# Three changes of order in a cross-attention and feed-forward kernel: weight requests ahead of context, six high halves on VectorE, first maxima earlier

## The reference, cut to what matters

```python
def reference(x, ctx, pweight, nweight, exps, bexps, mask_weight, scale, pbias, nbias, biasscale):
    x = x + attention(layernorm(x), ctx, ctx)        # causal, 16 heads, scale 1/8
    soft = sigmoid(pweight) - sigmoid(nweight)       # (1024, 1024, 4)
    weight = einsum('oin,n->oi', soft, exps * sigmoid(mask_weight)) * scale
    bias = quantised(einsum('on,n->o', pbias - nbias, bexps)) * biasscale
    return x + layernorm(x) @ weight.T + bias
```

## Time and profile before

| | us |
|---|---|
| median of 3 runs | 1187.38 (1184.31 to 1188.52) |
| the profiled execution, its own time | 1185.72 |
| its span | 1183.9 |
| TensorE busy | 1098.5 (93%) |
| VectorE busy | 994.4 (84%) |
| ScalarE busy | 862.3 (73%) |
| GpSimd busy | 492.7 (42%) |
| SyncE's transfers, share of 16 DMA engines | 70.4% |

### The profile page before, as it was taken

How to read it: one execution, slowest core, us unless ns; L and a number is a source line. 1 busy time by engine, 2 the same in 40 slices (tenths; PEclk the granted TensorE clock), 3 DMA queues, 4 the chain that set the end, 5 groups by cost and what they waited for, 6 DMA issues and landing times.

```text
span 1183.9 us, 32049 instructions
## 1 busy us (share of the span) xinstructions
PE 1098.5 (93%) x13092; PEld 808.7 (68%) x13092; DVE 994.4 (84%) x1552; ACT 862.3 (73%) x1770; POOL 492.7 (42%) x510
## 2 busy tenths in 40 slices
PE   3778888999999999999999999999999999999988
PEld 3666665666766777777776777777776676777753
DVE  5765688899988988998988888999988888998962
ACT  5887865777786777778776777777786777877740
POOL 3343534433334754344235654343335655331150
PEclk9999999999999999999999999999999999999999
DMA  8999936577659877775678887667768976654443
GB/s 308 301 295 337 299 80 120 134 146 122 151 121 186 189 180 131 162 160 112 132 121 203 194 173 148 139 140 130 137 125 205 185 171 131 137 117 86 89 90 71
DMA packets 382594, 191.13 MB, mean 161 GB/s; under 512 B 358128, under 2 KB 358128, under 8 KB 378352
## 3 DMA queue, kind: packets, MB, share of 16 engines
q1 hardware_dynamic: 381440, 189.05, 70.4%
q10 hardware_dynamic: 1008, 0.04, 0.1%
HBM read 67.15 MB, written 16.78 MB: 71 GB/s over the span
## 4 chain that ended last, share of the span: by engine, by line
PE 47%; DVE 18%; ACT 14%; DMA 7%; issue 7%; SPq 4%; POOL 3%; ACTq 0%; POOLq 0%; DVEq 0%
PE ffnb L468 15%; PE ptb L429 8%; PE slot L415 5%; PE slot L416 5%; DVE pd L656 4%; ACT p L537 4%; DVE mx L642 4%; DMA pd<-pd 4%; ACT pd L546 4%; PE obank L449 4%; ACT pt L553 4%; PE obank L452 3%; DVE stats L674 3%; PE obank L450 3%; DVE pt L648 3%
## 5 line engine op out<-in xcount | busy, mean ns | idle before, releaser
L537 ACT ACTIVATE p<-slot,mx 128x512 f32<-128x512 f32 (+7 forms) x512 | 377.4, 745 | 135.1 <-issue 71.2
L642 DVE TENSOR_REDUCE mx<-slot 128x1 f32<-128x640 f32 (+7 forms) x352 | 356.0, 1014 | 32.0 <-PE slot L419 31.3
L468 PE MATMUL ffnb<-wt,yt 128*128 128x512 f16 x1464 | 372.1, 380 | 1.1 <-DMA yt<-y 0.8
L648 DVE SCALAR_TENSOR_TENSOR pt<-ptb,pt 128x512 f16<-128x512 f32 (+1 forms) x504 | 281.6, 598 | 51.8 <-ACT pt L553 50.3
L553 ACT ACTIVATE pt<-ptb 128x512 f16<-128x512 f32 (+1 forms) x504 | 239.9, 526 | 106.0 <-PE ptb L429 104.8
L415 PE MATMUL slot<-kt,qt 128*128 128x128 f16 (+3 forms) x1056 | 267.2, 283 | 14.0 <-ACT p L537 5.9
L416 PE MATMUL slot<-kt,qs 128*128 128x128 f16 (+3 forms) x1056 | 267.2, 283 | 0.0
L870 POOL TENSOR_TENSOR ring<-ring,att 128x256 f32<-128x256 f32 x128 | 94.2, 736 | 394.0 <-DVE att L667 393.9
L429 PE MATMUL ptb<-id,p 128*128 128x128 f32 x1700 | 238.3, 279 | 10.9 <-DVE pt L648 10.8
L468 PEld LDWEIGHTS ffnb<-wt,yt 128*128 128x128 f16 x1464 | 137.2, 98 | 100.1 <-issue 2.2
L449 PE MATMUL obank<-v,pt 128*128 128x64 f16 x1700 | 176.9, 193 | 16.3 <-DVE att L667 12.1
(11 more groups left out here) (92 smaller groups left out, 1528.7 us busy)
## 6 DMA issues: line engine op xcount, KB each, us to landing
ring<-in_x_dram SPq DMA_DIRECT2D x32, 512.0 KB, 4.5
cin<-in_ctx_dram SPq DMA_DIRECT2D x32, 512.0 KB, 4.9
out_dram<-ring SPq DMA_DIRECT2D x32, 512.0 KB, 3.3
qs<-qt SPq DMA_DIRECT2D x124, 128.0 KB, 2.9
v<-in_weights_dram SPq DMA_DIRECT2D x11, 1024.0 KB, 8.1
kt<-in_weights_dram SPq DMA_DIRECT2D x11, 1024.0 KB, 8.0
pd<-in_weights_dram SPq DMA_DIRECT2D x5, 1024.0 KB, 7.3
yt<-in_weights_dram SPq DMA_DIRECT2D x5, 1024.0 KB, 10.0
```

Of the source, the lines that this page charges most:

```text
L468: last = pe.matmul(dst, yt[:, k % 2, a * KT_N + kk, :], wt[:, c, kk, half * 512:half * 512 + 512], start=r == 0, stop=r == 3 * KT_N - 1)
L537: last = nc.scalar.activation(p32[:, j.par, hh * j.keys:(hh + 1) * j.keys], slot[:, j.par, base:base + j.keys], ACT.Exp, bias=mx[:, j.par, ...
L642: nc.vector.tensor_reduce(mx[:, j.par, 0:j.heads], src[:, 0:j.heads, 0:j.keys], AX_X, ALU.max, negate=True).then_inc(mx_ready, 1)
L648: nc.vector.scalar_tensor_tensor(pt[:, j.par, j.blocks + blocks.start:j.blocks + blocks.stop, :], ptb[:, c % 2, 0:P * len(blocks)].rearran ...
```

## The change

It does three things. SyncE asks for a step's two chunks of weights before it asks for the context (and so also before turn_k), not after. For tiles 2, 3 and 4, VectorE writes the high halves of context and query itself, directly before the low halves, where ScalarE wrote them one or two steps earlier. In the prologue, ScalarE does the context's high half before the tanh of chunk 0, and takes the exponentials of job 0 before the query's high half and those of job 1 before the tanh of chunk 1; VectorE takes the maxima of job 0 before the context's low half, and those of job 1 before the query's.

```diff
+def high_on_dve(t):
+
+    return 1 < t < 5
...
                     if s == LOADS[n][0] and t + 3 < TILES:
                         load_x(t + 3)
+                    u = FIRST[t] + s + PAIRS // 2
+                    if u < UNITS:
+                        load_w(2 * u)
+                        load_w(2 * u + 1)
                     if s == LOADS[n][1] and t + 3 < TILES:
                         load_c(t + 3)
...
                     if s == turn_k_step(t) and t + 2 < TILES:
                         turn_k(t + 2)
-                    u = FIRST[t] + s + PAIRS // 2
-                    if u < UNITS:
-                        load_w(2 * u)
-                        load_w(2 * u + 1)
...
+            c_split(1)
             chunk_tanh(0)
-            c_split(1)
+            exponentials(JOBS[0])
             q_split(1)
+            exponentials(JOBS[1])
             chunk_tanh(1)
-            exponentials(JOBS[0])
-            exponentials(JOBS[1])
...
-                if s == C_HI[steps(t)] and t + 2 < TILES:
+                if s == C_HI[steps(t)] and t + 2 < TILES and not high_on_dve(t + 2):
                     c_split(t + 2)
-                if q_at(t, s, 2):
+                if q_at(t, s, 2) and not high_on_dve(t + 2):
                     q_split(t + 2)
...
             def q_split(t):
+                if high_on_dve(t):
+                    dve.wait_ge(q_norm, t + 1)
+                    dve.wait_ge(q_in[(t - 1) % 2], 16 * by_dma(t - 1))
+                    nc.vector.tensor_copy(q16[:, :, 0:D], norm32[:, :].rearrange("p (h d) -> p h d", d=D)
+                                          ).then_inc(q_hi, 1)
                 dve.wait_ge(q_hi, t + 1)
...
             def c_split(t):
+                v = v16[:, t % V_PLACES]
+                if high_on_dve(t):
+                    dve.wait_ge(c_in, 16 * (t + 1))
+                    nc.vector.tensor_copy(v[:, :, 0:D], cin[:, :].rearrange("p (h d) -> p h d", d=D)).then_inc(c_hi, 1)
                 dve.wait_ge(c_hi, t + 1)
...
+            maxima(JOBS[0])
             c_split(1)
+            maxima(JOBS[1])
             q_split(1)
-            maxima(JOBS[0])
-            maxima(JOBS[1])
             first_difference(0)
```

More of the change, by code:

```diff
@@ L692, in c_split @@
             def c_split(t):
+                v = v16[:, t % V_PLACES]
+                if high_on_dve(t):
+                    dve.wait_ge(c_in, 16 * (t + 1))
+                    nc.vector.tensor_copy(v[:, :, 0:D], cin[:, :].rearrange("p (h d) -> p h d", d=D)).then_inc(c_hi, 1)
                 dve.wait_ge(c_hi, t + 1)
-                v = v16[:, t % V_PLACES]
                 nc.vector.tensor_tensor(v[:, :, D:2 * D], cin[:, :].rearrange("p (h d) -> p h d", d=D),
```

## The result

| | before | after |
|---|---|---|
| median of the runs taken side by side, us | 1187.38 (1182.95 to 1188.95, 5 runs) | 1179.2 (1177.64 to 1184.74, 5 runs) |
| the profiled execution, its own time | 1185.72 | 1179.6 |
| its span | 1183.9 | 1177.8 |
| ratio after to before | | 0.9943, 95% interval 0.9921 to 0.9966 |

The changed kernel is 0.57% faster, 6.8 us with an interval of 4.0 to 9.4. The prediction was 1183.2, 4.2 us faster, which lies inside this interval. The two profiled spans are 6.1 us apart.

The account below looks back on a forecast made before the run. Bound: the saturated transfer queue with ScalarE nearly full at 76 to 142 us, TensorE from 200. Queue 2.3 + casts 1.9 + prologue and copies 0 = 4.2 us, giving 1183.2 from 1187.38; own range 1181.5 to 1185.0, wide 1180.0 to 1187.8.

Parts of the forecast that it names:

- That the stage decides and the rest follows: Weights stage, to about 150 us: ending it earlier moves all later work equally, so a gain there counts at the end.
- The prologue, 0: Prologue's new order: tile 2's load of x doesn't move, so earlier exponentials are waited off; 0, with 1 us either side.
- moments before 35 us: VectorE's moments of x of tile 2, at 36.01 before; starting before 35 us would prove the prediction wrong on the fast side.
- A transpose holds SyncE for the queue's sake, not for its own: SyncE's turn_k and turn_q: long durations of 7.25 to 11.03 us are the queue draining; an empty queue takes 1.78 us.
- The slower rival: Job 7: transposes keep their long times whatever is queued, chunk 22 is asked for later; 4.9 us slower, 1192.3, chance 0.09.
- The queue's gain, 2.3 us: Weights asked for ahead of context: chunks 22 and 23 gain what the saturated transfer queue gains, 2.3 us, bounds 0 and 5.7.
- two holes: Transfer queue empty about 1.3 us at 52 us, and about 1.0 us lost at 96 to 98 us inside a transpose.
- The wait for chunk 22: ScalarE, with stalls before chunks 18 to 21 gone, would wait the longer for chunk 22; its tanh near 109.4 us.
- The casts, 1.9 us from tile 4 and nothing from tiles 2 and 3: High halves moved to VectorE: tile 4's two save 2 x 0.95 us on the chain; the earlier four only lengthen ScalarE's wait.
- The copies meet GpSimd: Tile 4's copies on VectorE wait out a GpSimd neighbour, overdrawing their cover by about 1.4 us each; gain 1.4, 1186.0, chance 0.05.
- the wide range: Whole-kernel time of 1180.0 to 1187.8 us, taking in all cases but the fastest and slowest rivals, 0.17 together.
- the queue stops deciding: Before chunk 22: all four ScalarE stalls go (5.7 us) and four casts pay 0.95 each; 9.5 us, time 1177.9, chance 0.08.
- The chance of faster, 0.5: Whole kernel: 0.42 from the forecast gaining beyond about 0.3% (3.6 us), plus 0.08 from the fastest rival.

Follow-up runs that it names:

- the repeat: The changed kernel run again with no edit, against the kernel before: 0.9944 (0.9923 to 0.9966), 6.6 us faster.
- the filled kernel before: The kernel before plus idle matmuls ahead of TensorE's wait in units 1, 3 and 11, against the kernel before: 0.9971, 3.4 us faster.
- the full order: Kernel before with SyncE asking for weights ahead of both load_c and turn_k (jobs 2, 3, 6, 7, 12); alone, against the kernel before: 0.9967, 3.9 us faster.
- the kernel with jobs 2, 6 and 12: Kernel before with weights asked for ahead of load_c only, turn_k still ahead of them in jobs 3 and 7: 0.9963, 4.4 us faster.
- job 2 alone: Kernel before with weights asked for ahead of load_c in job 2 only, against the kernel before: 0.9989 (0.9973 to 1.0004), 1.3 us.
- the filled one: The changed kernel plus idle matmuls ahead of TensorE's wait in units 1, 3 and 11, against the kernel before: 0.9947, 6.3 us faster.
- jobs 6 and 12: Kernel before with weights asked for ahead of load_c in these two jobs only, against the kernel before: 1.0 (0.9989 to 1.0012), 0.

## Why the prediction was right or wrong, point by point

**That the stage decides and the rest follows: right.** 7.5 us won at the start of the linear layer, 6.1 in the span, the difference within the scatter of the rest. In the profile of the repeat it was 5.0 and 3.8.

**The prologue, 0: right** within its bound of 1 us (0.5 by itself, and 1 us between the kernels with and without it). The load of x of tile 2 swallowed it as the chain of waits said: from the copy of qs to the moments of tile 2 it is 18.4 to 19.6 us in the five profiles with the new order of the prologue and 18.0 to 19.3 in the eight with the old one and no filling (20.5 in the filled kernel before). The forecast had named moments before 35 us as a sign that it was wrong on the fast side. They came at 34.35 and 34.24, and the sign misled: the copy of qs had come as much earlier, ahead of the change.

**A transpose holds SyncE for the queue's sake, not for its own: right.** turn_k(2) started at 58.38 (57.5 forecast) and took 6.29 us, turn_q(2) behind it 1.82; in the other profiles with the full order they took 5.0 to 8.4 and 1.6 to 3.1. The slower rival, which needed 9 us, is out. This was the reading on which the sign hung, and one row, the 1.78 us of a transpose in an empty queue, decided it rightly against four long ones.

**The queue's gain, 2.3 us: direction right, size probably too small.** SyncE's order alone measured 3.9 us (1.5 to 6.3), so 2.3 is inside the interval, but the term is the likeliest to be short. Chunk 22's tanh starts 5.0 us earlier with it, 5.7 and 2.2 in the two profiles of the changed kernel. I had counted two holes, 1.3 us at 52 and 1.0 at 96. The first agrees with the measurements: the exchange came 1.5 us earlier in the kernel with jobs 2, 6 and 12, and job 2 alone gave 1.3 us. The second, between the transposes of tile 3, was narrowed and not closed. What I left out may be a thin stretch behind turn_k(2), in the kernel before's own windows:

```profile
61.00:62.00 1.00, 1.00 (x6) 0.89 (x5) 0.97 (x4) 1.00 (x1) 0.48 (x2) 1.00 0.74 26
64.00:65.00 1.00, 1.00 (x12) 0.97 (x11) 1.00 (x3) 1.00 (x3) 0.00 (x0) 1.00 0.92 100
```

While SyncE is inside a transpose it asks for nothing else, and in these rows the queue moves 26 and 100 GB/s at a share that looks nearly busy. I had looked for low shares and not for low rates. With the pair side by side I would expect one such stretch and not two, and the exchange after turn_q(2) seems to show it: 69.18, 69.36, 69.83, 69.87 and 68.55 us in the five profiles with the full order and no filling (72.35 in the filled one, whose unit 3 was late), 73.26, 74.58 and 73.25 in the three with the old order. That is some 4 us, where I had 1.3. But two results stand against this as the reason of the gain. The kernel with job 2 alone has its exchange at 69.30 with the transposes apart, and was 1.3 us faster; and the kernel with jobs 2, 6 and 12 keeps them apart as well and was 4.4 us faster, as much as the full order. So where the rest beyond my 2.3 us came from stays open. The measured facts are that it needs no neighbouring transposes, that 1.3 us (job 2) and 0 (jobs 6 and 12) don't add up to it, and that with TensorE's idle stretches filled the whole change is worth 2.9 us only. I had put nothing in the sum for TensorE's clock.

The wait for chunk 22 didn't grow either, as I had written that it would: it was 2.21 us before and 1.44 and 2.25 in the changed kernel.

**The casts, 1.9 us from tile 4 and nothing from tiles 2 and 3.** By themselves they measured 0.5 us (-1.3 to 2.4); on top of the new order the two repeats differ by 2.7 (6.6 less 3.9, with the prologue in it), with intervals of more than 2 us each. Both hold 1.9 and neither shows it. That tiles 2 and 3 add little agrees with 5.9 against 6.6 us, whose intervals allow some 3 us either way, and with the wait for chunk 22. The copy I took at 0.65 us was 0.68 to 0.69, and it hid: VectorE's waits for ScalarE in the places of tile 4 shrank from 1.99 and 1.25 us to 0.31 and 0.52.

**The copies meet GpSimd: didn't happen.** All six took 0.68 or 0.69 us in the first profile, and none of them overlapped an instruction of GpSimd there, so what a meeting would cost isn't measured. (By its own terms, 2.3 + 0.65 less 1.25 of cover, the price of a meeting is 1.7 us, not 1.4. And the 2.75 us that stood for it is a difference of two inputs, which ran beside GpSimd's; it says nothing certain of a copy with one input.)

**The forecast as a whole.** Direction, path and the main mechanism (SyncE's order) were right. The sum was 2.6 us below the measured 6.8 and inside its interval. Of the 2.6, 1.6 are the difference of the queue's term to its own measurement (3.9), and the rest can't be placed: the three parts alone gave 3.9, 0.5 and 0.5 us, together 4.9. The forecast's own range, 1181.5 to 1185.0, was too narrow: the ratio of 0.9943 makes 1180.6 of the 1187.38 before, inside the wide range, and the median of 1179.2 lies 0.8 us below that range too. So the wide range held by little. The rival "the queue stops deciding" (1177.9) had foreseen two stalls that did vanish, but chunk 22 was waited for in every profile, and its 9.5 us are just outside the interval. The chance of faster, 0.5, hung on a forecast placed just beside the line of 0.3%.

## What to carry to other kernels

When one engine issues both loads and transposes, it stands inside a transpose until what was queued ahead has drained (here 5 to 11 us against 1.8 with an empty queue). Put requests whose place is already free ahead of any wait: that gave 4.4 us here. Putting the transposes next to each other shortened the second to some 2 us in the queue, but gave nothing that the device time could tell. Look for holes of a queue by its rate as well as by its busy share. Relieving an engine that shares a stage with a full queue may show little: here the casts gave 0.5 us alone. And before a gain is put down to the order of a queue, repeat the comparison with TensorE's idle stretches filled: here it fell from 6.6 to 2.9 us.

## What the runs showed of the hardware

TensorE's granted clock was 0.50 (1.2 GHz) in short stretches of this stage, mostly behind 2.5 to 4.7 us of idle time (but unit 3 of the kernel before ran at full clock behind 2.88), and in a different place from one execution to the next: the sums of units 1, 10 and 11 in the kernel before, of 1, 3 and 11 in the changed one, of 3 and 11 in its second profile. Such a unit takes 5.2 to 6.7 us instead of 3.7. One window of the changed kernel, on unit 3:

```profile
54.00:55.00 1.00, 1.00 (x3) 0.78 (x3) 1.00 (x3) 1.00 (x5) 0.85 (x2) 0.50 0.98 406
```
 
I hadn't expected that much of the scatter between runs may hang on it: with 100 small matmuls in three idle stretches the kernel before became 0.29% faster and its scatter shrank from 6.9 us (27 runs) to 1.5 (9 runs). The runs of the kernel before point the same way. Of the 85 that were timed beside the experiments, the eight with a mean granted clock of 0.981 took 1188.16 to 1191.13 us, the four with 0.991 1181.42 to 1187.16. That the filling acts through the clock is shown for unit 11 and argued for the rest. A float32 to float16 cast of 128x1024 took VectorE 0.68 to 0.69 us and ScalarE 1.03 to 1.07.
